# A two-layer decoder: t rounded by VectorE, and the five FFN maxima turned by TensorE

## The reference

```python
def act_qdq(x):                       # one scale for the whole tensor
    qmax = 2.0 ** 15 - 1.0
    scale = jnp.maximum(jnp.max(jnp.abs(x)) / qmax, 1e-12)
    return jnp.clip(jnp.round(x / scale), -qmax - 1.0, qmax) * scale
x = act_qdq(x)
up = act_qdq(x @ lpbq_dequant(w_up).T)
gate = act_qdq(x @ lpbq_dequant(w_gate).T)
sig = fixed_qdq_u16(jax.nn.sigmoid(gate))
gate = act_qdq(gate * sig)            # this one is called t in the kernel
o = act_qdq(gate * up)                # and this one v
return o @ lpbq_dequant(w_down).T
```

## Time and profile before

| what | value |
|---|---|
| median of three runs | 1464.83 us |
| profiled execution, its own time | 1464.9 us |
| span of the profile | 1463.1 us |
| PE busy | 1287.1 us (88%) |
| PE weight load busy | 877.9 us (60%) |
| DVE (VectorE) busy | 1037.6 us (71%) |
| ACT (ScalarE) busy | 517.5 us (35%) |
| POOL (GpSimd) busy | 277.1 us (19%) |
| mean granted TensorE clock | 0.938 |

### The profile page before, as it was taken

How to read it: one execution, slowest core, us unless ns; L and a number is a source line. 1 busy time by engine, 2 the same in 40 slices (tenths; PEclk the granted TensorE clock), 3 DMA queues, 4 the chain that set the end, 5 groups by cost and what they waited for, 6 DMA issues and landing times.

```text
span 1463.1 us, 17935 instructions
## 1 busy us (share of the span) xinstructions
PE 1287.1 (88%) x7132; PEld 877.9 (60%) x7132; DVE 1037.6 (71%) x1974; ACT 517.5 (35%) x602; POOL 277.1 (19%) x188
## 2 busy tenths in 40 slices
PE   7899999997789999856467999999999999998964
PEld 4566777765644454323345586776867686766653
DVE  4678888885344579967635487887879797878684
ACT  2333333332224567677211233222332323241310
POOL 0111111111000000027100041413223041414141
PEclk9999999996689999978688999999999999999997
DMA  4000000000152045499431202111111000000000
GB/s 191 15 15 30 30 29 15 30 15 0 58 217 101 29 152 192 131 327 325 153 110 41 92 3 68 42 55 55 51 48 62 30 22 19 27 24 28 0 15 15
DMA packets 47059, 104.66 MB, mean 72 GB/s; under 512 B 10496, under 2 KB 31104, under 8 KB 43648
## 3 DMA queue, kind: packets, MB, share of 16 engines
q1 hardware_dynamic: 42816, 101.42, 19.7%
q10 hardware_dynamic: 4160, 2.10, 0.5%
HBM read 59.47 MB, written 44.04 MB: 71 GB/s over the span
## 4 chain that ended last, share of the span: by engine, by line
PE 75%; DVE 13%; ACT 6%; issue 3%; DMA 1%; POOL 1%; SPq 0%; POOLq 0%; DVEq 0%; ACTq 0%
PE ps L1147 7%; PE ps L1207 7%; PE ps L1036 6%; PE ps L872 6%; PE ps L923 5%; PE ps L809 5%; PE ps L716 4%; PE ps L1180 3%; PE ps L1094 2%; PE ps L825 2%; PE ps L789 2%; PE ps L1118 2%; PE ps L1129 2%; PE ps L1224 2%; PE ps L1027 2%
## 5 line engine op out<-in xcount | busy, mean ns | idle before, releaser
L1207 PE MATMUL ps<-arena 128*128 128x256 f32 x512 | 119.8, 388 | 6.7 <-ACT arena L1603 6.7
L1630 POOL TENSOR_TENSOR arena<-arena 128x4 f32<-128x4 f32 x48 | 49.2, 1025 | 369.8 <-DVE arena L1790 369.8
L1147 PE MATMUL ps<-arena 128*128 128x512 f32 x256 | 117.6, 598 | 0.0
L1207 PEld LDWEIGHTS ps<-arena 128*128 128x128 f32 x512 | 98.4, 194 | 28.0 <-ACT arena L1603 10.2
L1036 PE MATMUL ps<-arena 128*128 128x256 f32 x384 | 89.5, 393 | 22.4 <-DVE arena L2051 20.2
L2096 DVE TENSOR_TENSOR arena<-ps,arena 128x2048 f32<-128x2048 f32 x32 | 73.3, 2292 | 39.4 <-PE ps L1094 39.1
L1694 POOL TENSOR_TENSOR arena<-arena 128x16 f32<-128x16 f32 x32 | 92.1, 2913 | 34.1 <-DVE arena L2125 34.1
L1036 PEld LDWEIGHTS ps<-arena 128*128 128x128 f32 x384 | 75.0, 198 | 33.7 <-issue 20.6
L872 PE MATMUL ps<-arena 128*128 128x512 f32 x192 | 85.3, 601 | 1.2 <-ACT arena L1322 1.2
L923 PE MATMUL ps<-arena 128*128 128x512 f32 x192 | 85.0, 595 | 1.4 <-ACT arena L1348 1.4
L809 PEld LDWEIGHTS ps<-arena 128*128 128x128 f32 x512 | 66.4, 209 | 17.9 <-ACT arena L1295 15.3
(11 more groups left out here) (246 smaller groups left out, 2649.9 us busy)
## 6 DMA issues: line engine op xcount, KB each, us to landing
v_scratch<-arena SPq DMA_DIRECT2D x7, 1536.0 KB, 8.5
arena<-v_scratch SPq DMA_DIRECT2D x7, 1536.0 KB, 6.7
up_scratch<-arena SPq DMA_DIRECT2D x6, 1536.0 KB, 7.3
arena<-up_scratch SPq DMA_DIRECT2D x6, 1536.0 KB, 9.4
arena<-x_scratch SPq DMA_DIRECT2D x16, 512.0 KB, 3.9
vw_scratch<-arena SPq DMA_DIRECT2D x32, 256.0 KB, 4.7
arena<-vw_scratch SPq DMA_DIRECT2D x8, 1024.0 KB
arena<-x SPq DMA_DIRECT2D x8, 512.0 KB, 4.2
```

The costliest lines, as they stand in the source:

```text
L1147: last = mm(flat(p % 2), w["cos_wq"][:, k, p * P:(p + 1) * P], xt4[:, k], start=k == 0, stop=k == NC - 1)
L1207: last = mm(flat(2)[:, C:2 * C], cos_pt[:, p], cos_vw[:, par, p], start=p == 0, stop=p == NP - 1)
L1630: g.tensor_tensor(var[0], var[1], neghalf[:, 0:NT], ALU.pow)\
```

## The change

Two edits, both in the FFN of layer 0.

First, t is rounded by VectorE. `ffn_round_t` and its eight calls leave ScalarE's order; `product(q)` begins with a tensor_scalar from f32 to int16 on VectorE in place of its wait for ScalarE, and VectorE waits for that rounding's own completion before it multiplies.

Second, the maxima no longer go through GpSimd. VectorE's `peak` spreads the column of maxima over a new 128x128 tile `spread`; TensorE turns that tile into a PSUM bank, which puts all 128 maxima into every partition; VectorE's `scale` begins with a tensor_reduce over 128 columns of that bank. `share_peak` stands in TensorE's order: for x behind the last turn of the weights, for gate behind `metric_products` and ahead of the first up pass, for up ahead of `values(3)`, for t between `value_products(6)` and `value_products(7)`, and for v behind the last wait on the keys. TensorE also waits for the scale of gate ahead of `spec_forward` and for that of t ahead of `key_rows(0)`, since these write the banks that the maxima were read from. VectorE's `peak` waits until the preceding maximum has been shared, since the tile is used again. Tiles behind `spread` in the arena move by 128 words.

```diff
+        spread = ar.take(P)
...
-        ar.at = values_at - 2 * NC * P
+        ar.at = values_at - 2 * NC * P - P
...
+        PEAK_BANK = {"x": 7, "gate": 7, "up": 2, "t": 3, "v": 2}
...
             pe.wait_ge(ev("weight_copied"), WEIGHTS["w_down"])
+            def share_peak(name, k):
+                pe.wait_ge(ev("peak_found"), QUANTIZED[name])
+                tr(flat(k)[:, 0:P], spread, ident).then_inc(ev("peak_shared"), 1)
+            share_peak("x", PEAK_BANK["x"])
...
             def spec_forward():
                 wait(pe, "gate_copied", Batch(B - 1), NF, NF)
+                pe.wait_ge(ev("scale_ready"), QUANTIZED["gate"])
...
                     wait(pe, "up_copied", Batch(B - 1), NF, NF)
+                    pe.wait_ge(ev("scale_ready"), QUANTIZED["t"])
...
             metric_products()
+            share_peak("gate", PEAK_BANK["gate"])
             up_pass(0, after=(spec_forward,))
...
+            share_peak("up", PEAK_BANK["up"])
             values(3)
             value_products(6)
+            share_peak("t", PEAK_BANK["t"])
             value_products(7)
             values(4)
...
             pe.wait_ge(ev("cos_k_scaled"), 4)
+            share_peak("v", PEAK_BANK["v"])
             pe.wait_ge(ev("scale_ready"), QUANTIZED["v"])
...
-            def ffn_round_t(q):
-                if q == 0:
-                    act.wait_ge(ev("scale_ready"), QUANTIZED["t"])
-                wait_back(act, "v_ready", Batch(q), 2)
-                f(t_i[:, q % 2], gated[:, V_ORDER[q]], ACT.Copy, scale=quant["t_mult"])\
-                    .then_inc(sig("t_rounded").sem, 1)
...
             ffn_round_up(0)
             ffn_round_up(1)
-            ffn_round_t(0)
             copy_vw(7)
             copy_values(4)
-            ffn_round_t(1)
             ffn_round_up(2)
             copy_vw(8)
             ffn_round_up(3)
             copy_keys(0)
-            ffn_round_t(2)
...
-            def share_peak(name):
-                pool.wait_ge(ev("peak_found"), QUANTIZED[name])
-                g.partition_all_reduce(quant[name + "_all"], quant[name + "_max"], P, bass.bass_isa.ReduceOp.max)\
-                    .then_inc(ev("peak_shared"), 1)
-            share_peak("x")
             pool.wait_ge(ev("null_k_floored"), 1)
             g.tensor_tensor(null_n, null_n, neghalf[:, 0:1], ALU.pow).then_inc(ev("null_k_rnormed"), 1)
-            share_peak("gate")
...
-            share_peak("up")
-            share_peak("t")
...
-            share_peak("v")
+            pool.wait_ge(ev("peak_found"), QUANTIZED["v"])
             wait_all_moved(pool, "v_stored", 4, 3)
...
             def peak(name):
-                v.tensor_copy(quant[name + "_max"], quant[name + "_max"]).then_inc(ev("peak_found"), 1)
+                if QUANTIZED[name] > 1:
+                    dve.wait_ge(ev("peak_shared"), QUANTIZED[name] - 1)
+                v.tensor_copy(spread, quant[name + "_max"].broadcast_to([P, P])).then_inc(ev("peak_found"), 1)
...
                 dve.wait_ge(ev("peak_shared"), QUANTIZED[name])
+                link(v.tensor_reduce(quant[name + "_all"], flat(PEAK_BANK[name])[:, 0:P], AX.X, ALU.max))
...
             def product(q):
                 at = V_ORDER[q]
-                wait(dve, "t_rounded", Batch(q))
+                link(v.tensor_scalar(t_i[:, q % 2], gated[:, at], quant["t_mult"], None, ALU.mult))
                 wait(dve, "up_rounded", Batch(q))
```

More of the change, by code:

```diff
@@ L1501, in _ @@
             copy_keys(1)
-            ffn_round_t(3)
             copy_vw(10)
@@ L1508, in _ @@
             copy_values(6)
-            ffn_round_t(4)
             copy_vw(12)
@@ L1515, in _ @@
             copy_values(7)
-            ffn_round_t(5)
             copy_vw(14)
@@ L1520, in _ @@
             copy_vw(15)
-            ffn_round_t(6)
             store_keys(3)
-            ffn_round_t(7)
             wait_all_moved(act, "v_stored", 4, 3)
```

## The result

The changed kernel took 1469.69 us (median of 17 runs), the kernel before 1465.9 (17 runs): ratio 1.0026, 95% interval 1.0015 to 1.0036. That is 3.8 us slower, clear of the noise and within the 0.5% that the prediction called no change. Forecast was +1.4, in a range of 1461.5 to 1471.5. The profiled execution took 1468.45; its span is 3.54 longer than that of before.

What follows compares the result with a forecast made beforehand. TensorE was taken as three quarters of the chain, with a ring from product to product ordering the product stage. -2.03 + 1.97 + 0.9 + 0.54 = +1.4 on 1464.9 gave 1466.3 us, range 1461.5 to 1471.5.

Steps and rivals of the forecast that it cites:

- layer 1 as unchanged: Layer 1, whose instructions are the same, keeps its length; a changed length would make the prediction wrong.
- x, -2.03: Joint of x: the scale starts at 400.90 instead of 402.93, 2.03 us saved; a late clock could take up to 1.0.
- rival F: Joint of x: the pause stays because something other than the reduce makes it; +2.0, 1468.3 us; chance 0.03.
- gate, +1.97: Joint of gate: the turn stands behind layer-1 products, so ScalarE's work comes 1.97 us later, on the chain.
- Rival A: Behind gate: the clock falls in TensorE's new pause, costing 2.0 us more, 1468.3 us; chance 0.17.
- up and t, +0.9 at the last product: Product stage: waiting for up's maximum delays TensorE and ScalarE; last product starts at 707.35 against 706.42, 0.9 us lost.
- the ring: Product stage: product-to-product chain through ScalarE, GpSimd and VectorE, now including t's rounding; 12.49 us for each of three turns.
- Rival B: Product stage: GpSimd's power step is kept out until the product ends; +1.0 three times, 1469.3 us; chance 0.15.
- D: Product stage: t's rounding runs at one column a cycle (3.36 us); 11.4 us slower, 1477.7 us; chance 0.06.
- E: Product stage: keys are never late and VectorE is the bound; -8.5, 1456.4 us; chance 0.04.
- C: Joint of up and t: `values(3)` runs at the full clock and nothing is late; -1.5, 1464.8 us; chance 0.13.
- v, +0.54: Joint of v: 0.71 us becomes 1.25, 0.54 lost, bounds 0.3 to 0.8, all on the chain.

Runs made afterwards that it cites:

- a4: The changed kernel with gate's maximum back on GpSimd; 1468.81 us, ratio 1.0021.
- d2: The changed kernel unchanged, traced a second time; 1469.11 us, ratio 1.0014.
- a1: The kernel before with only the rounding of t moved to VectorE, all maxima staying with GpSimd; 1464.91 us, ratio 0.9996.
- b7: a1 with VectorE's rounding of t done twice in front of each product; 1479.59 us, ratio 1.0096.
- b6: a1 with the rounding of t(q+1) issued directly behind product q, ahead of the key sum; 1468.19 us, ratio 1.0014.
- c1: The kernel before with only an unused tile of 128 words put in front in the arena; 1464.0 us, ratio 0.9989.
- d3: The kernel before with six one-column copies on VectorE ahead of the maximum of v; 1468.66 us, ratio 1.002.
- d4: The kernel before with twelve one-column copies on VectorE ahead of the maximum of v; 1469.54 us, ratio 1.002.
- a3: The kernel before with only x's maximum turned by TensorE, new tile and waits included; 1467.1 us, ratio 1.0015.
- a2: The changed kernel with t rounded by ScalarE as before, so only the five maxima are moved; 1469.25 us, ratio 1.0036.
- c2: a3 with the new tile at the arena's end, so that no other tile moves; 1468.95 us, ratio 1.0017.

## Why the prediction was right, and where it was off

The forecast of no change and its range held. It is 2.4 us short in the medians (+3.8 against +1.4), because its sum took layer 1 as unchanged, and layer 1 lost 2.8. That the part ahead of layer 1 came out near the forecast (+1.2 against +1.4) is in part luck: the term of x was 0.88 too good, the term of the product stage 0.95 too bad.

- **x, -2.03.** The joint fell by 2.25; copy 0.23 and reduce 0.29 against 0.28 each, so rival F is out. Of this 1.10 went back through the lower clock, a little over the "up to 1.0" that the step named and did not put into the sum. That was the wrong value: the row showed the turns at the lower clock already, and nothing in it said that the clock would rise earlier. Mis-sized: -1.15 in place of -2.03.
- **gate, +1.97.** +1.80, by the mechanism described: the turn came behind the layer-1 products. Rival A (a lower clock behind the pause) did not come about: 3.70 for eight products, both times. But a4 shows that the step is worth less than it reads: without it, the up passes lose the same amount elsewhere.
- **up and t, +0.9 at the last product.** `values(3)` took 3.22 at the lower clock (3.06 forecast). `value_products(6)` then ran in 1.13, not in 2.08. This is the term that was wrong: TensorE had the higher clock again by 624.60. Product 0 started at 629.65 (629.8), product 1 at 638.49 (638.6), product 2 at 652.04 (652.2). That these times fit is luck: the stage started 0.92 later than before's, which the forecast left out, and `value_products(6)` was 0.95 shorter. Measured from its own start the stage costs -0.05 instead of +0.9. What holds the first keys was named rightly. The first store of v was issued at 634.72, 2.5 earlier than before, but took 11.0 in place of 7.3 and landed at 645.7 (645.9 forecast); the copy of the keys started at 645.75. ScalarE's rounding ahead of it, held for 2.68 by a store of the values' products [L1412 above], ended at the same time, so this trace does not separate the two; in d2 ScalarE stood idle for 0.24 and started its copy as the store landed (647.1).
- **the ring.** 12.49 forecast, 12.49, 12.47, 12.62 measured; 8.83 forecast, 8.84 and 8.83 measured; the rounding 1.81. a1 and b7 confirm its composition: 1.85 more per turn for one more rounding. Rival B (GpSimd kept out until the product ends) is out in this order, with 4.41 for the power step, and b6 shows it where the rounding does not precede the product. D (a slow rounding) is out with 1.81, E (VectorE the bound) too, since VectorE waits 10.6 for GpSimd's squares and is busy 75.88 of 89. The clock of C did not come for `values(3)`, only behind it.
- **v, +0.54.** +0.47.
- **what was missing: +2.8 in layer 1.** This is the step that failed: the prediction took layer 1's length as unchanged, left it out of the sum, and named its change as what would make it wrong. The windows of before could have warned: its layer 1 starts at a granted clock of 0.76 (720 to 740) and has 0.91 in the fill, so its length could depend on when it starts. a1 and c1 keep the 54.6, every kernel with a turn at x loses it, but so do b6 without such a turn and d3; and d4, with nothing but a delay, is as late at the third residual sum as they are. So a later start alone can lengthen layer 1: by 2.9 in the fill of d3, by 0.7 in that of d4, whose whole loss of 4.2 is 1.9 more than its delay. The change starts layer 1 1.2 later. That this delay, and nothing else, makes its 2.8 is argued from these and from the order of the table; no run had a delay of that size alone. That the granted clock makes the difference is shown by the rows; why it falls where it does stays open, and the profile of before alone could not have told on which side of such a step the change would end. The range could have held one more "up to" for this stretch.

Counted from the maximum of x in the profiled executions, the change is 1.2 behind at the down product, 0.3 at the second residual sum and 3.1 at the third.

## What to carry to other kernels

Cost a joint by what stands ahead of it in the order of the engine that is to serve it: the same turn took 1.03 where TensorE was free and 2.5 behind its queue, against 0.71 for a collective step whose engine had nothing else to do. Moving work off an engine that the next engine waits for brings nothing where both stand in one ring; add up the ring, and double one member to see whether it counts. Where a pipeline's start runs at a mixed clock, a shift of some tenths of a microsecond can go with a loss of three in work that was not edited (0.3 in a3). So put such stretches into the range, and follow a gain to the end of the trace before you believe it.

## What the hardware showed that was not expected

- Kernels whose layer 1 started 0.3 to 2.3 us late all reached its third residual sum 2.97 to 3.11 late, in unchanged work (eight traces; 2.97 where nothing but a delay of 2.3 was put in). Those up to 0.1 late lost nothing. The lengths repeat: 54.64 and 54.64, 57.42 and 57.45 in two executions each.
- The last batches have such a step of their own: behind the sixth spectral sum after, b6, a2, a4 and d2 lose 0.3 up to the end of the span, but a3, c2, b7, d3 and d4 lose 1.1 to 1.2 with the same instructions (granted clock over 1380 to 1410: 0.85 in a3, 1.00 in after). Why, no run shows.
- Three kernels whose ScalarE began rounding gate 1.1 earlier than before (a3, a4, c2) lost 1.8 to 2.0 in the up passes, 108 us of nearly gapless products, 1.7 of it in the same 24 (10.57 to about 12.27), in a3 at a mean clock of 0.98.
- VectorE and GpSimd keep each other out in both directions: the rounding, 1.82 alone, took 3.42 beside a GpSimd square of 1.90, and the power step took 2.90 where it started first, 4.41 behind the start of a rounding, 6.00 behind that of a product. In after a waiting step got in between two VectorE operations 0.03 us apart (652.01 and 652.04).
- The first partition_all_reduce costs 3.28 from column to scale at x (before) and 0.71 at gate, where GpSimd had been idle for 30.15 (a3).
